# An attention block with a mixture of experts on one core: the row sums of a quarter gathered on GpSimd, two output banks, and a wider-spaced order

## The reference

```python
xn = layernorm(x)                                   # x is (4, 1024, 512), float32
q, k, v = (proj(W, b) for W, b in ...)              # 16 heads of 32
scores = einsum('bhqd,bhkd->bhqk', q, k) / sqrt(32)
scores = where(causal, -inf, scores) + alibi_bias
probs = softmax(scores, axis=-1)
out = einsum('bhqk,bhkd->bhqd', probs, v) @ Wo.T + bo
...
logits = einsum('th,eh->te', xn, gate_w)            # 8 experts, top 2 of 8 per token
act = silu(g) * u                                   # g, u from w1, 352 wide
expert_out = einsum('eti,ehi->eth', act, w2)
return x + out + moe(xn)
```

## Time and profile before

| what | value |
|---|---|
| median of 3 runs | 1602.4 us |
| the profiled execution | 1602.33 us, span 1600.5 us |
| PE busy | 1447.4 us (90%) |
| DVE busy | 897.5 us (56%) |
| POOL busy | 878.1 us (55%) |
| ACT busy | 705.4 us (44%) |
| granted TensorE clock, mean | 0.965 |

### The profile page before, as it was taken

How to read it: one execution, slowest core, us unless ns; L and a number is a source line. 1 busy time by engine, 2 the same in 40 slices (tenths; PEclk the granted TensorE clock), 3 DMA queues, 4 the chain that set the end, 5 groups by cost and what they waited for, 6 DMA issues and landing times.

```text
span 1600.5 us, 35240 instructions
## 1 busy us (share of the span) xinstructions
PE 1447.4 (90%) x13499; PEld 868.3 (54%) x13499; DVE 897.5 (56%) x1741; ACT 705.4 (44%) x1179; POOL 878.1 (55%) x756
## 2 busy tenths in 40 slices
PE   4689979999998999998999889896789999999995
PEld 2456646554555654555556456652356656566663
DVE  7666766665576665766658796670143333333332
ACT  5235555545556554555655444464122222222221
POOL 5134555546457354545645446657307677777764
PEclk9899999999998999999999999997899999999998
DMA  7245432534533436344143410115787788888784
GB/s 251 48 133 132 137 106 70 132 114 147 145 100 97 118 107 191 100 119 131 42 130 100 129 47 16 41 50 178 278 207 123 135 133 132 132 133 148 135 128 53
DMA packets 189308, 193.92 MB, mean 121 GB/s; under 512 B 104899, under 2 KB 138947, under 8 KB 189020
## 3 DMA queue, kind: packets, MB, share of 16 engines
q1 hardware_dynamic: 160636, 152.27, 35.8%
q0 software_dynamic: 26128, 37.24, 13.8%
q10 hardware_dynamic: 2384, 2.16, 0.4%
HBM read 93.14 MB, written 53.74 MB: 92 GB/s over the span
## 4 chain that ended last, share of the span: by engine, by line
PE 66%; DVE 8%; POOL 7%; SPq 6%; DMA 6%; issue 4%; ACT 2%; ACTq 0%; POOLq 0%; DVEq 0%
PE S L1349 16%; PE O L1277 6%; SPq L1047 5%; PE S L1198 4%; PE O L1380 4%; PE M L1380 4%; DVE arena L1658 3%; PE S L1259 3%; PE T L1215 3%; PE T L1198 3%; PE O L1287 3%; PE T L1231 2%; PE S L1231 2%; DMA arena<-in_x 2%; POOL arena L1971 2%
## 5 line engine op out<-in xcount | busy, mean ns | idle before, releaser
L1851 ACT ACTIVATE arena<-S,psl 128x512 f32<-128x512 f32 (+1 forms) x640 | 401.1, 643 | 353.4 <-PE S L1261 178.0
L1971 POOL TENSOR_TENSOR arena<-arena 128x1024 f32<-128x1024 f32 (+1 forms) x160 | 316.7, 1980 | 155.0 <-ACT arena L1851 154.9
L2025 POOL DMA_INDIRECT out<-arena x142 | 221.6, 1561 | 108.1 <-issue 43.0
L1349 PE MATMUL S<-arena 128*128 x1704 | 265.7, 312 | 4.3 <-DVE arena L1756 2.0
L1349 PEld LDWEIGHTS S<-arena 128*128 128x128 f16 x1704 | 166.2, 98 | 100.8 <-issue 5.6
L1658 DVE TENSOR_REDUCE arena<-T 128x1 f32<-128x512 f32 (+3 forms) x241 | 156.2, 654 | 92.7 <-PE T L1236 53.7
L1658 DVE TENSOR_REDUCE arena<-S 128x1 f32<-128x512 f32 (+3 forms) x256 | 167.0, 657 | 72.3 <-PE S L1236 39.3
L1259 PE MATMUL S<-arena 106*128 106x256 f16 x640 | 178.5, 279 | 27.5 <-ACT arena L1851 27.0
L1277 PE MATMUL O<-arena 128*32 128x256 f32 (+1 forms) x2560 | 160.5, 369 | 0.8
L1960 POOL TENSOR_TENSOR arena<-arena 128x512 f16<-128x512 f32 x64 | 77.4, 1210 | 140.5 <-DVE arena L1631 140.2
L1770 DVE COPY arena<-T 128x512 f16<-128x512 f16 x71 | 30.2, 425 | 215.0 <-PE T L1364 209.2
(11 more groups left out here) (235 smaller groups left out, 2528.3 us busy)
## 6 DMA issues: line engine op xcount, KB each, us to landing
arena<-arena SPq DMA_DIRECT2D x192, 128.0 KB, 2.4
arena<-in_w1T SPq DMA_DIRECT2D x64, 352.0 KB, 3.5
arena<-in_x SPq DMA_DIRECT2D x64, 256.0 KB, 4.0
w_d<-arena SPq DMA_DIRECT2D x32, 352.0 KB, 2.8
arena<-w_d SPq DMA_DIRECT2D x16, 704.0 KB, 6.6
arena<-in_w2T SPq DMA_DIRECT2D x32, 256.0 KB, 2.9
out<-arena SPq DMA_DIRECT2D x32, 256.0 KB, 2.4
xn_d<-arena SPq DMA_DIRECT2D x24, 256.0 KB, 2.1
```

The costliest lines, as they stand in the source:

```text
L1349: tp = pe.matmul(y[:, i * 512:i * 512 + I], xT[:, s % XDEEP, 4 * a + c, :], weights[:, bass.ds(reg[s] + (w_ * NX * W1N + c * 2 * I + i * I ...
L1851: act.activation(PT[t % 3][:, h, 0:n], CB[o.bank["score", u]][:, 0:n], ACT.Exp, scale=psl[:, hh:hh + 1]).then_inc(sems["exp"], 1)
L1971: pool.tensor_tensor(PS[t % 2][:, :, f:f + n], PT[t % 3][:, :, f:f + n], PT[t % 3][:, :, c:c + n], ALU.add).then_inc(sems["add"], 1)
L2025: pool.indirect_dma_start(out=halves, out_offset=bass.IndirectOffsetOnAxis(row[:, part, s:s + 1].bitcast(U32), 0), in_=yo[:, s % YDEEP, c0 ...
```

## The change

Five things change together.

1. The row sums. POOL no longer adds only the two key tiles of a quad. It keeps one sum PS for the whole quarter: in quarter 0 a copy of 4 x 128 columns and an addition of 4 x 128; in the first quad of the others one addition of 1024 columns, and in every further quad two additions, which have a wait between them. PE makes one row-sum product a quarter (four matmuls of 256 columns). There are three buffers PS, and `exp` no longer waits for `rsum`.
2. Two output banks. `pv` and `rsum` of a quarter go alternately to O and M; PB keeps four banks.
3. The order. Every `pv` stands at unit 4t + 5 (before: 4t + 7 or 4t + 8 where i = 0), `rsum` at 4t + 10, `bc` nine units after `osb` in place of six, `mtr` three units after the last maximum in place of one, the maxima begin 5 units later and wait in the plan for their stack, and the `stack` DMAs of a group go out one head every two units.
4. The low halves `xnl` of batches 1 to 3 move from POOL to DVE.
5. The residual of the output projection gets four buffers (eight in the last batch), is loaded earlier, and `xbo` stands six units behind its load. The last weight window waits for the last store. The routing starts 10 units earlier.

```diff
-        self.size = {"S": 2, "O": 1, "X": 2, "Y": 2, "C": 2}
+        self.size = {"S": 2, "O": 2, "X": 2, "Y": 2, "C": 2}
...
-            at(4 * t + (8 if (q, i) == (1, 0) else 7 if i == 0 else 5), lambda: products(t))
+            at(4 * t + 5, lambda: products(t))
             if i == q:
-                at(4 * t + (9 if q == 0 else 8), lambda: sums(t))
+                at(4 * t + 10, lambda: sums(t))
...
     def products(t):
         G, q, i = quad(t)
-        if i:
-            sums(t - 1)
-        else:
+        if i == 0:
             o.take("O", "pv", G, q)
         add("pv", t)
...
         at(now[0] + 3, inverse)
-        at(now[0] + 6, spread)
+        at(now[0] + 9, spread)
...
-        add("oload", b, i, sem=f"res{out_slot(b, i)}", inc=16)
-        add("xbo", b, i)
+        add("oload", b, i, sem=f"res{min(out_slot(b, i), 4)}", inc=16)
+        at(now[0] + 6, lambda: add("xbo", b, i))
...
-    PB = [*TB, GU[0][:, 0:512], GU[0][:, 512:1024], MB]
+    PB = [*TB, GU[0][:, 0:512], GU[0][:, 512:1024]]
...
                 for x in range(4):
-                    R = OB[D * x:D * x + D, 2 * P:4 * P]
-                    if i < q:
-                        tp = pe.matmul(R, ones, PS[t % 2][:, x, :], start=False, stop=False)
-                    else:
-                        pe.matmul(R[:, 0:P], ones, PT[t % 3][:, x, 0:P], start=False, stop=False)
-                        tp = pe.matmul(R[:, P:2 * P], ones, PS[t % 2][:, x, P:2 * P], start=False, stop=True)
+                    tp = pe.matmul(YB[o.bank["pv", G, q]][D * x:D * x + D, 2 * P:4 * P], ones, PS[(4 * G + q) % 3][:, x, :],
+                                   start=False, stop=True)
...
+                if q == 0:
+                    pool.tensor_copy(z[:, :, 0:P], y[:, :, 0:P])
+                    pool.tensor_tensor(z[:, :, P:2 * P], y[:, :, P:2 * P], y[:, :, 2 * P:3 * P], ALU.add).then_inc(sems["add"], 1)
+                elif i == 0:
+                    pool.tensor_tensor(z, y[:, :, 0:2 * P], y[:, :, 2 * P:4 * P], ALU.add).then_inc(sems["add"], 1)
+                else:
+                    on.wait_ge(*at("add", t - 1))
+                    then(pool.tensor_tensor(z, z, y[:, :, 0:2 * P], ALU.add))
+                    f, c, n = (0, 2 * P, 2 * P) if i < q else (P, 2 * P, P)
+                    pool.tensor_tensor(z[:, :, f:f + n], z[:, :, f:f + n], y[:, :, c:c + n], ALU.add).then_inc(sems["add"], 1)
```

More of the change, by code:

```diff
@@ L190, in ln_tile @@
         add("xnh", b, half, i)
-        add("xnl", b, half, i)
+        if b:
+            at(now[0] + 1, lambda: add("xnl", b, half, i))
+        else:
+            add("xnl", b, half, i)
     turned = {}
@@ L208, in ln_gate @@
     def ln_gate(b):
+        while turned.get((b, 1, 3), 1 << 30) >= now[0]:
+            yield 0
         yield from lock(("gate", b))
@@ L275, in stack_when @@
             yield 0
-        stack(b, g)
-        yield 0
+        for _ in stack(b, g):
+            yield 0
+            yield 0
     def qkv_steps(b, g):
@@ L298, in rest @@
                     add("join", G, q, sem="mx")
-                at(now[0] + 1, row)
+                at(now[0] + 3, row)
         def row():
@@ L337, in sums @@
         add("rsum", t)
-        if i == q:
-            at(now[0] + 1, lambda: emptied(G, q))
+        at(now[0] + 1, lambda: emptied(G, q))
     def emptied(G, q):
@@ L382, in rest @@
                     o.give(key, ("y", b, i))
-                    n = 6 if b == B - 1 else 2
-                    at(now[0] + 1, lambda: add("ostore", b, i, sem=f"yd{out_slot(b, i)}", inc=16))
-                    if i + n < 8:
-                        at(now[0] + 4, lambda: o_load(b, i + n))
+                    at(now[0] + 1, lambda: add("ostore", b, i, sem=f"yd{min(out_slot(b, i), 4)}", inc=16))
+                    if i + 4 < 8 and b < B - 1:
+                        at(now[0] + 4, lambda: o_load(b, i + 4))
                 later.append(rest)
@@ L498, in routing @@
         add("listr")
+        for i in range(4, 8):
+            o_load(B - 1, i)
         yield
@@ L521, in ln_steps @@
             yield from ln_stats(b, half)
-            for _ in range(3):
+            for _ in range(8):
                 yield 0
@@ L598, in plan @@
             if i == 15:
-                stack(0, 0)
+                for _ in stack(0, 0):
+                    pass
                 add("place", 1, sem="pos0", inc=16 * 2)
@@ L655, in plan @@
                 fill.append((first + k, last + (8, 18, 30, 46)[i // 2], proj_o(b, i)))
-        for i in range(6 if b == B - 1 else 2):
-            at(u0 + 126, lambda b=b, i=i: o_load(b, i))
+        for i in range(4):
+            at(u0 + 112, lambda b=b, i=i: o_load(b, i))
         if b + 1 < B:
-            pace.append((u0 + 70, 1, ln_steps(b + 1)))
+            pace.append((u0 + 65, 1, ln_steps(b + 1)))
             fill.append((u0 + 101, u0 + 112, ln_gate(b + 1)))
@@ L664, in plan @@
     split_jobs = [w_max(), w_scales(), w_split()]
-    pace.append((40 * 11 + 24, 2, routing()))
+    pace.append((40 * 11 + 14, 2, routing()))
     pace.append((40 * 15 + 24, 1, first_slots()))
@@ L684, in plan @@
             f()
-        for n in due.pop(u, []):
-            maxima(n)
+        wanted += due.pop(u, [])
+        for _ in range(2):
+            if wanted and ready.get(("stack", *divmod(wanted[0] // len(PIECES), NG)), u) < u:
+                maxima(wanted.pop(0))
         if u >= 4 and not (u < 160 * (B - 1) and 70 <= u % 160 < 104):
@@ L887, in build @@
     AFTER_PT = to
-    zeros, to = place(to, [P, E], F32)
+    PS2, to = place(to, [P, 4, 2 * P], F32)
     V1, to = place(to, [P, 8, P], F32)
@@ L904, in build @@
     to = max(to, EARLY1 + WEND)
-    res, to = place(to, [P, 2, E], F32)
+    res, to = place(to, [P, 4, E], F32)
+    zeros = res[:, 3, :]
     LATE = to
@@ L1127, in sync @@
                     on.wait_ge(*at("bc", GROUPS - 1, 3))
-                    for i in range(2, 6):
-                        on.wait_ge(*at("ostore", B - 1, i))
+                    on.wait_ge(*at("ostore", B - 1, 7))
                 for f, n, d, i, x in pieces(LOW[key[0]], LOW[key[0] + 1]):
@@ L1544, in vector @@
                                   ALU.mult).then_inc(sems["xn"], 1)
+            elif kind == "xnl" and key[0]:
+                b, half, i = key
+                k = half_place(*key)
+                on.wait_ge(*at("xnh", *key))
+                dve.tensor_tensor(XH[k][:, E:2 * E], x_place(b, half, i), XH[k][:, 0:E],
+                                  ALU.subtract).then_inc(sems["xnl"], 1)
             elif kind == "tops":
@@ L1881, in scalar @@
                 on.wait_ge(*at("rsum", 10 * G + (0, 2, 5, 9)[q]))
-                act.activation(osb[:, q % 2, :], OB[:, :], ACT.Copy).then_inc(sems["osb"], 1)
+                act.activation(osb[:, q % 2, :], YB[o.bank["pv", G, q]][:, :], ACT.Copy).then_inc(sems["osb"], 1)
             elif kind == "wsh":
@@ L1946, in gpsimd @@
                 pool.tensor_scalar(w, r, XS, None, ALU.mult).then_inc(sems["newton"], 1)
-            elif kind == "xnl":
+            elif kind == "xnl" and not key[0]:
                 b, half, i = key
@@ L2022, in gpsimd @@
                 else:
-                    for i in range(2, 8):
+                    for i in (0, 1, 2, 3, 7):
                         on.wait_ge(*at("ostore", B - 1, i))
```

45 lines of the change are left out of this document (21 added, 24 removed).

## The result

| | before | after |
|---|---|---|
| median, us (4 runs each, taken together) | 1602.83 | 1634.42 (1632.31 to 1637.48) |
| ratio, 95% interval | | 1.0202 (1.0175 to 1.0228) |
| profiled execution, span | 1602.33, 1600.5 | 1634.51, 1632.6 |
| granted clock, mean | 0.965 | 0.946 |

The kernel is 32 us slower. The forecast was 1516 us in 1477 to 1585, so the sign is wrong. The "slower" rival named almost the right time, 1631 us, but another place, so its number is luck.

The account below looks back on a forecast made before the run. PE was taken to set the pace in attention (busy 964.45 of 1052 us). 1602.3 - 57 (row sums) - 22 (order, banks, new waits) - 15 (clock) + 8 (DVE) + 0 (passage) = 1516 us, range 1477 to 1585.

Parts of the forecast that it names:

- "slower" rival: Attention: POOL sets the pace and PE waits at each of the 64 products; 115 us, 1631 us; chance 0.07.
- Row sums on PE: Attention: 64 row-sum products, 33.9 us, in place of 94.4 us, relieve PE of 60.5 us; less a sixteenth, -57 us.
- Additions on POOL: Attention: 96 more full additions take POOL from 557.7 to about 773 us; late additions cost some 20 us.
- Order and banks: Attention: PE waits of 47 us go; new waits of 25 (POOL 20, fourth lent bank 5) come: -22 us net.
- DVE, "which has the room": Attention: DVE near 705 of 966 us; slower splits beside POOL add 15 us of DVE, which has the room.
- The low halves, +8: Attention: 24 low halves moved to DVE add 17 to 28 us of its time; +8 us in the sum.
- The clock, -15: Attention: if half of the long gaps go, a good third of 42 us comes back: -15 us, bounds 0 and 42.
- The passage, 0 in -5 to +7: Between attention and experts: later product +2.6, slower gathering +3, faster steps behind it -5.4: 0 us, between -5 and +7.
- POOL sets the pace everywhere: Attention: in-order and with port conflicts, POOL makes PE wait at each of 64 products; 1631 us; chance 0.07.
- The products were not on the path: Attention: PE idles where the products stood, since exponentials and maxima come no sooner; time stays at 1602; chance 0.04.

Follow-up runs that it names:

- b: The changed kernel with row sums as before (one addition and one product a quad), everything else changed: 1591.2 us, ratio 0.9940 to the kernel before.
- g: The changed kernel with the additions of quads 0 < i < q left out, one product a quarter kept: 1572.1 us, ratio 0.9810 to the kernel before.
- i: As g, but with five POOL writes of a constant in place of the additions left out: 1603.6 us, ratio 1.0008 to the kernel before.
- c: The changed kernel with the low halves xnl of batches 1 to 3 back on POOL: 1630.1 us, ratio 1.0175 to the kernel before.
- j: The changed kernel with row sums as before and xnl back on POOL: 1585.5 us, ratio 0.9902 to the kernel before.
- k: The changed kernel with 96 row-sum products put back on PE, waiting for nothing of POOL: 1650.1 us, ratio 1.0290 to the kernel before.
- a: The kernel before with only the quarter sums on POOL and one row-sum product a quarter: 1643.7 us, ratio 1.0244 to the kernel before.

## Why the prediction was wrong

The miss of 118 us lies almost wholly in attention, forecast at 966 and measured at 1073. By the three parts, with the forecast's terms put to them: gaps forecast at 74, measured 123, **+49**; the clock's loss forecast at 13, measured 49, **+36**; work forecast at 879, measured 901, **+22**.

By the experiments: the sums were forecast at -57 for the products and +10 for waits at them (20, less the 9.9 of today), -47 us, and they cost 43. The rest (waits -37 and +5, clock -15, low halves +8) was forecast at -39, and b gives -11. That is 90 and 28 of the 118. The 90 are three steps: the 57 us taken at full length, 19 measured, **38**; POOL's occupation, 10 forecast and 31 measured, **21**; the standstills of DVE, priced at nothing, 31 measured, **31**. So the first and the third are the steps that failed. One by one:

- **Row sums on PE, -57.** Wrong was first to carry it into the sum as time: the bare removal gave 19 us (b to g). The work was too large as well, 43 to 46 us measured. An off-diagonal product was counted at 0.53 us, 0.65 less a slot of 0.12. But 0.20 us of it pass before the product's first matmul (640.12 to 640.32), and they stay, since the product with V behind it now has them (below, 645.23 to 645.43). What goes is 640.77 - 640.32 = 0.45 us, 96 times, 43 us. The 64 products that stay go from 0.80 to 0.77 us (646.78 to 647.55), 2 us.

```profile
645.23 0.27 PE L1268 MATMUL S<-arena 106*128 106x256 f16 x1
645.43 1.07 PE L1284 MATMUL O<-arena 128*32 128x256 f32 x16
...
646.78 0.27 PE L1268 MATMUL S<-arena 106*128 106x256 f16 x1
646.98 0.64 PE L1292 MATMUL M<-arena,cF 128*32 128x256 f32 x8
647.55 0.34 PE L1238 MATMUL S<-arena 105*128 105x384 f16 x1
```

- **Additions on POOL.** The load was forecast at 773 us and is 769, an instruction at 2.413 us and is 2.412. The new wait at the product, forecast at 20 us, is 9.1 us in 5. But i against g shows that the occupancy cost 31 us all the same.
- **Order and banks, -22 net.** Right in the comparison that isolates it: without the waits at the product, -37 and +5, and with the +8 of the low halves, gaps should have fallen by 24 us in b and fell by 21. What b lacks of its 39 us lies elsewhere: the clock's loss fell by 6 us and not by 15, the work came out 8 us higher, and passage and experts are 6 us longer. The waits for DMA fell from 25.2 to 5.5 us. The fourth bank, set at 5 us, costs the kernel before 6 to 9.
- **DVE, "which has the room".** This step failed. I forecast 705 us of 966; it was 770 of 1073. The stretching was seen and one line was sized about right (the split at "near 1.5 us", measured 1.54). The error was twofold: I applied it to that line alone and not to the norm's scaling and the additions of eight columns, which grew by 33 us, and I priced it as load on an engine with room. Its price is the delay of what stands behind it: PE's waits for DVE went from 14.3 to 61.8 us, and those for ACT, which waits for the scaling, from 27.0 to 45.0. Not all of that is the reading: waits for DVE are 20.9 us in b, 36.1 in g and 42.3 in i. The rule and the row stood in the prediction, and no term of the sum came from them.
- **The low halves, +8.** c and j bear out 4 to 6 us.
- **The clock, -15.** Wrong in sign. I coupled it to the forecast gaps, and the gaps grew. But in g the loss rose from 22 to 45 us with the gaps only 8 us higher, so another part is not from longer gaps. The 42 us that I started from were too many: PE was busy in 56 of the 75 us at the lower clock, and half of that is 28.
- **The passage, 0 in -5 to +7.** Measured +6.6: the product comes 6.5 us later behind the last score, the gathering is slower by 3.4 us, as weighed, and the steps behind it are 3.4 us faster, where 5.4 was forecast. Half of it is the order's: b's passage is already 3 us longer than before.
- **The rivals.** "POOL sets the pace everywhere" gave 1631 us with port conflicts, at PE's waits for the 64 products. The size is right by luck, the place wrong: PE waits at 5 products. The conflict strikes at DVE, two engines away from the wait. "The products were not on the path" had 0.04; k shows that a good half of it is true once the additions are in.

Open remains why PE's time at the lower clock rises when the products go. In attention it is 75 us before, 48 in b, 101 in g, 106 in i and 130 after. The place is known: of the 53 us from b to g, 51 lie in groups 2, 6, 10 and 12, whose gaps rose only from 28 to 39 us; in group 2 the granted clock is 0.95 in b and 0.82 in g. These four groups became 18 us longer by the bare removal, while the other twelve became 33 us shorter. With the products put back into the changed kernel (k) it is 112 us in place of 130; in g this was not tried. The experts' stage is 3.2 us longer than before. It is so in b too (3.3 us) and not in a, so it comes with the order and the banks; how is open.

## What to carry to other kernels

Work moved to GpSimd costs by what its reads do to the in-order list of VectorE, not only by its own waits: list every VectorE instruction with two operands in SBUF or a long tensor-scalar one in SBUF, assume that each may last one GpSimd addition longer (the split, 0.74 us at its shortest, reached 3.08), and look at what stands behind it. Take an order and an offload apart before judging either: here the order alone gained 11 us (16 with the low halves left where they were) and was hidden behind a loss of 43. Time removed from the engine that is busy 92% is worth its full length only while its suppliers keep up; here some 46 us removed gave 19.

## What the runs showed of the hardware

A VectorE addition of 128 x 8, 166 ns at its shortest, lasted up to 2329 ns beside GpSimd's additions:

```profile
L1672 DVE TENSOR_TENSOR arena<-arena x32: 166/394/2329, 78.4 to 1115.2; 128x8 f32<-128x8 f32 x32
L1546 DVE TENSOR_SCALAR arena<-arena,mv,nw x32: 527/589/2582, 12.7 to 791.7; 128x512 f32<-128x512 f32 x32
```

A tensor-scalar instruction with one tensor in SBUF is stretched as well (527 to 2582 ns). GpSimd's writes of a constant, 0.965 us for 128 x 1024, stretch it only as far as they last: with 240 of them and the same busy time the scaling had a mean of 934 ns, against 887 without them and 1307 beside the additions, and 11 of its 32 instances ended 0.28 us behind a write. The additions of 8 columns, with two operands in SBUF, were no longer beside these writes than without them (means of 435 and 520 ns, against 781 beside the additions). A GpSimd addition of 1024 columns takes 2.41 us and four of 256 columns take 3.1 us.
